# A shifted-window attention block: q and k parts in two buffers, another order of copies on SyncE's queue, and a maximum where a cast was

## The reference

```python
y = _ln(x, norm1_g, norm1_b)
y = jnp.roll(y, (-SS, -SS), axis=(1, 2))          # windows of 7 x 7 are cut from this
qkv = yw @ qkv_w.T + qkv_b
attn = jnp.einsum('bhqd,bhkd->bhqk', q * scale, k) + bias + mask
attn = softmax(attn)
o = jnp.einsum('bhqk,bhkd->bhqd', attn, v)
o = o @ proj_w.T + proj_b                         # back to the image, rolled back
x = shortcut + o
h = gelu(_ln(x, norm2_g, norm2_b) @ fc1_w.T + fc1_b)
return x + h @ fc2_w.T + fc2_b
```

## Time and profile before

| | |
|---|---|
| time, median of 3 runs (lowest to highest) | 5146.63 us (5140.37 to 5152.69) |
| the profiled execution | 5130.69 us, its span 5128.9 us |
| busy share of PE, PEld, DVE, ACT, POOL | 77%, 60%, 58%, 55%, 58% |
| mean granted clock of TensorE | 0.917 |
| SyncE's DMA queue | 429.09 MB, 38.9% of 16 DMA engines' time |
| one stack fill, one load of x | 196.0 KB each |
| the two copies of the row sums | 24.5 KB each |

### The profile page before, as it was taken

One profiled execution on the slowest core, in us unless ns is written; L12 is line 12 of the kernel. 1 busy time (PEld: TensorE's weight loads), 2 busy tenths in 40 slices (PEclk: granted clock), 3 DMA queues, 4 the chain that ended last, 5 costly groups with the idle time before them and its releaser, 6 DMA issues. The chain is left out here.

```text
span 5128.9 us, 216807 instructions
## 1 busy us (share of the span) xinstructions
PE 3941.8 (77%) x96144; PEld 3081.9 (60%) x96144; DVE 2974.2 (58%) x7839; ACT 2821.6 (55%) x3840; POOL 2995.4 (58%) x3983
## 2 busy tenths in 40 slices
PE   3777787777777787777777777778777877787777
PEld 2566666656666665665666666656666666666565
DVE  4555555556556555555555555555555555556564
ACT  1555555555555555555555555555555555555554
POOL 1566566566656656655655555566556555555665
PEclk9899989999999989999999989999999899899999
DMA  3443443444344344434433443444344334333432
GB/s 89 87 89 83 93 89 85 87 92 89 83 96 90 81 88 91 89 81 94 89 85 85 93 88 83 89 91 89 81 95 90 84 85 93 85 88 87 93 86 58
DMA packets 595395, 447.85 MB, mean 87 GB/s; under 512 B 125703, under 2 KB 594039, under 8 KB 594447
## 3 DMA queue, kind: packets, MB, share of 16 engines
q1 hardware_dynamic: 591979, 429.09, 38.9%
q10 hardware_dynamic: 2064, 3.21, 0.2%
q0 software_dynamic: 416, 1.68, 0.1%
HBM read 109.49 MB, written 51.46 MB: 31 GB/s over the span
## 5 line engine op out<-in xcount | busy, mean ns | idle before, releaser
L609 DVE TENSOR_REDUCE neg_max<-ps 113x16 f32<-113x784 f32 x1024 | 999.5, 976 | 723.7 <-PE ps L769 631.4
L430 ACT ACTIVATE probs<-ps,own 113x784 f32<-113x784 f32 x1024 | 917.7, 907 | 642.6 <-PE ps L801 586.0
L398 POOL TENSOR_TENSOR hid_lo<-probs,hid_hi 128x784 f16<-128x784 f32 x512 | 879.0, 1738 | 314.4 <-DVE hid_hi L603 314.4
L379 POOL TENSOR_SCALAR r_hi<-sums 128x98 f16<-128x98 f32 x128 | 175.2, 1368 | 1168.9 <-DVE sums L650 1168.9
L801 PE MATMUL ps<-st_q,st_k 127*49 127x49 f16 x32768 | 629.3, 186 | 130.6 <-issue 130.1
L801 PEld LDWEIGHTS ps<-st_q,st_k 127*49 127x49 f16 x32768 | 520.4, 103 | 216.7 <-issue 146.5
L492 ACT ACTIVATE k_hi<-ps,col 128x784 f16<-128x784 f32 x128 | 118.6, 926 | 927.8 <-DMA st_q<-q_lo 919.9
L769 PE MATMUL ps<-mx_k,mx_q 128*49 128x196 f16 x8192 | 546.1, 251 | 105.7 <-issue 43.8
L816 PE MATMUL ps<-probs,v_own 113*32 113x49 f32 x32768 | 515.1, 210 | 92.2 <-issue 61.3
L816 PEld LDWEIGHTS ps<-probs,v_own 113*32 113x32 f32 x32768 | 419.5, 110 | 206.2 <-issue 152.5
L848 PE MATMUL ps<-w_hi,hid_hi 128*112 128x128 f16 x3584 | 525.2, 226 | 12.9 <-issue 8.5
(11 more groups left out here) (112 smaller groups left out, 8710.0 us busy)
## 6 DMA issues: line engine op xcount, KB each, us to landing
st_k<-k_hi SPq DMA_DIRECT2D x256, 196.0 KB
st_q<-q_hi SPq DMA_DIRECT2D x256, 196.0 KB
oT_raw<-pv_sb SPq DMA_DIRECT2D x256, 196.0 KB, 6.0
x_in<-in_x SPq DMA_DIRECT2D x224, 196.0 KB
x_res<-in_x SPq DMA_DIRECT2D x224, 196.0 KB
out_y<-y_out SPq DMA_DIRECT2D x224, 196.0 KB
mx_k<-k_hi SPq DMA_DIRECT2D x512, 49.0 KB
mx_q<-q_hi SPq DMA_DIRECT2D x512, 49.0 KB
```

The source lines that it names most:

```text
L379: nc.gpsimd.tensor_scalar(r_hi[:, :, :], sums[:, :, :], 1.0, 0.0, ALU.mult, ALU.add).then_inc(s_r_hi, 1)
L398: nc.gpsimd.tensor_tensor(hid_lo[:, c, :], hid[:, c, :], hid_hi[:, c, :], ALU.subtract).then_inc(s_hid_lo, 1)
L430: nc.scalar.activation(probs[0:KP, w % 4, :].rearrange("p (b c) -> p b c", b=2), ps[0:KP, b:b + 2, 0:HB * WT], ACT.Exp, scale=own[0:KP, 2: ...
L609: nc.vector.tensor_reduce(neg_max[0:KP, :, w].rearrange("p (g e) -> p g e", g=GQ), ps[0:KP, 0:2, :].rearrange("p b (g c) -> p (b g) c", g= ...
```

## The change

Four edits:

1. `q_hi`, `q_lo`, `k_hi` and `k_lo` become two buffers each, used by turns. ScalarE's wait before `k_hi` now asks for the copies of the band before last.
2. On SyncE's queue, the last two stack fills move up behind the first four, ahead of the row sums.
3. The loads of x for band t + 3 move from behind the row sums to the end of the turn, behind the loads of `x_res`.
4. The high part of gelu's result, a cast by `tensor_copy`, becomes a `tensor_reduce` with maximum over an axis of one element, which rounds the same values to float16.

```diff
@@ buffers
-        q_hi, q_lo, k_hi, k_lo = (sb(n, [C, NW, 2, WT], F16) for n in ("q_hi", "q_lo", "k_hi", "k_lo"))
+        q_hi, q_lo, k_hi, k_lo = ([sb(f"{n}{e}", [C, NW, 2, WT], F16) for e in range(2)]
+                                  for n in ("q_hi", "q_lo", "k_hi", "k_lo"))
...
@@ SyncE
-                    fill(st_k, HIGH_ROWS, k_hi)
-                    fill(st_q, HIGH_ROWS, q_hi)
-                    fill(st_k, CROSS_ROWS[1], k_hi)
-                    fill(st_k, CROSS_ROWS[0], k_lo)
+                    fill(st_k, HIGH_ROWS, k_hi[odd(0)])
+                    fill(st_q, HIGH_ROWS, q_hi[odd(0)])
+                    fill(st_k, CROSS_ROWS[1], k_hi[odd(0)])
+                    fill(st_k, CROSS_ROWS[0], k_lo[odd(0)])
+                    fill(st_q, CROSS_ROWS[0], q_hi[odd(0)])
+                    fill(st_q, CROSS_ROWS[1], q_lo[odd(0)])
...
-                n = t + 3
-                if exists(n):
-
-                    sp.wait_ge(s_st1, n)
-                    if past(n, 1):
-                        sp.wait_ge(s_t1, n - 1)
-                    band_dmas(sp, xr, x_in[odd(3)], n, edge(n), False, s_x)
-                n = t
-                if exists(n):
-                    fill(st_q, CROSS_ROWS[0], q_hi)
-                    fill(st_q, CROSS_ROWS[1], q_lo)
...
                     band_dmas(sp, xr, x_res, n, edge(n), False, s_xres_dma)
+                n = t + 3
+                if exists(n):
+
+                    sp.wait_ge(s_st1, n)
+                    if past(n, 1):
+                        sp.wait_ge(s_t1, n - 1)
+                    band_dmas(sp, xr, x_in[odd(3)], n, edge(n), False, s_x)
...
@@ ScalarE
-                    if past(n, 0):
-                        act.wait_ge(s_mx_dma, N_MX * n)
-                        act.wait_ge(s_st_dma, N_ST * n)
-                    for j, (hi, bank, b) in enumerate(((k_hi, 0, BK), (q_hi, 6, BQ))):
+                    if past(n, 1):
+                        act.wait_ge(s_mx_dma, N_MX * (n - 1))
+                        act.wait_ge(s_st_dma, N_ST * (n - 1))
+                    for j, (hi, bank, b) in enumerate(((k_hi[odd(1)], 0, BK), (q_hi[odd(1)], 6, BQ))):
...
@@ VectorE, hid_high
-                nc.vector.tensor_copy(hid_hi[:, c, :], hid[:, c, :]).then_inc(s_hid_hi, 1)
+                nc.vector.tensor_reduce(hid_hi[:, c, :], hid[:, c, :].unsqueeze(2), AX_X, ALU.max).then_inc(s_hid_hi, 1)
```

More of the change, by code:

```diff
@@ L314, in body @@
                         sp.dma_start(mx_k[32 * e:32 * (e + 1):4, :, e, :],
-                                     k_hi[e:C:EQ, :, :, :].rearrange("c w m q -> c (w m q)")).then_inc(s_mx_dma, 16)
+                                     k_hi[odd(1)][e:C:EQ, :, :, :].rearrange("c w m q -> c (w m q)")).then_inc(s_mx_dma, 16)
                     sp.wait_ge(s_hi, 2 * n + 2)
@@ L318, in body @@
                         sp.dma_start(mx_q[edge(n)][32 * e:32 * (e + 1):4, :, :],
-                                     q_hi[e:C:EQ, :, :, :].rearrange("c w m q -> c (w m q)")).then_inc(s_mx_dma, 16)
+                                     q_hi[odd(1)][e:C:EQ, :, :, :].rearrange("c w m q -> c (w m q)")).then_inc(s_mx_dma, 16)
                 n = t - 3
@@ L657, in body @@
                 if exists(n):
-                    for j, (hi, lo, bank, b) in enumerate(((k_hi, k_lo, 0, BK), (q_hi, q_lo, 6, BQ))):
+                    for j, (hi, lo, bank, b) in enumerate(((k_hi[odd(1)], k_lo[odd(1)], 0, BK), (q_hi[odd(1)], q_lo[odd(1)], 6, BQ))):
                         dve.wait_ge(s_hi, 2 * n + j + 1)
```

## The result

| | before | after |
|---|---|---|
| median of the runs | 5149.15 us (5140.37 to 5152.69) | 5408.0 us (5403.5 to 5415.1) |
| profiled execution, span | 5130.69, 5128.9 us | 5415.1, 5413.3 us |
| mean granted clock of TensorE | 0.917 | 0.899 |

The ratio is 1.0507, with a 95% interval of 1.0488 to 1.0525. The forecast was 5255 us. The sign, the chain of waits and the range held. The size did not: about +106 us was forecast and +259 measured.

The account below looks back on a forecast made before the run. A cycle of waits repeated per band, no engine full. S 14.7 + 12.0 gives M 26.7 against 25.84: +0.86 us over 126 turns, +108 us, 5239 profiled, 5255 us median; range 5040 to 5435, with 50% on 5165 to 5360.

Parts of the forecast that it names:

- the chain of waits: Per turn: sums land later, q projection follows, one long TensorE pause, spread directly behind fc1, first row-maximum matmul behind x addition.
- The swap of waits: ScalarE's k_hi wait, 919.9 us, goes; the turn then depends on the row sums, delayed 3.8 us by two more fills.
- It is not the gain: Said of removing k_hi's 919.9 us wait: the rest of the turn passes from the last fill's landing to S.
- S: Moment VectorE gets the row sums, counted from the first fill's issue: 10.66 us before, 14.7 forecast.
- the late sums: Rival: row sums land at 16.1 us, +2.26 us a turn, 5431 us; chance 14%.
- the late turn: Second sample from the kernel before, no x left to load: 37.48 us long, S at 12.3, M at 24.0.
- x loaded last: x's two loads, 3.6 us, moved to the turn's end behind x_res: claimed to cost nothing and cover 3 us.
- S to M: From sums through q projection, spread and x addition to the first row-maximum matmul: 1.34 + 4.98 + 5.6 + 0.1 = 12.0 us.
- M: Start of the next band's first row-maximum matmul on TensorE, counted from first fill: 25.84 us before, 26.7 forecast.
- The rest of a turn: From M to the next turn's first fill: taken to follow M nearly one for one, 13.3 and 13.5 us.
- The sum: 14.7 + 12.0 = 26.7 against 25.84: +0.86 us a turn, +108 us over 126 full turns, 5255 us.
- The reduction: gelu's high part on VectorE: 976 ns against the cast's 569, 0.5 us lost there; GpSimd's r_hi 1.41 to 0.29 us.

Follow-up runs that it names:

- i_two_buffers: The kernel before with the second q and k buffers and the moved k_hi wait, nothing else: ratio 0.9651.
- d_single: The changed kernel with one buffer for each of the q and k parts and k_hi's old wait: ratio 1.0499.
- c_x_back: The changed kernel with the loads of x right behind the row sums again, as before: ratio 1.0218, 5246.66 us.
- e_oT_late: The changed kernel with the two output copies issued behind r_rows instead of right behind the sums: ratio 1.0358.
- m_x_last: i_two_buffers with the loads of x moved behind x_res as well: ratio 0.9842 to the kernel before.
- h_more_load: c_x_back with a further load of x's size behind x_res, into a buffer nobody reads: ratio 1.0380.
- b_cast: The changed kernel with gelu's high part as a cast again instead of the reduction: ratio 1.0497, 5385.59 us.
- a_sums_fifth: The changed kernel with the last two stack fills back behind the row sums, so four fills stand ahead: ratio 0.9858, 5059 us.
- j_split: The changed kernel with its queue reordered: two fills, sums, output copies, fills 3 and 4, maxima, r_rows, fills 5 and 6, x later: ratio 0.8534, 4386.67 us.
- p_split_cast: j_split with gelu's high part as a cast instead of the reduction: ratio 0.8533.
- k_four_early: j_split with fills 5 and 6 also ahead of r_rows: ratio 0.9577.

## Why the prediction was right in direction and wrong in size

- **The swap of waits: right.** k_hi's wait went, the sums' came, and TensorE's pause became a single long one before the q projection, half-clocked behind. i_two_buffers and d_single show both halves: the wait was worth 3.5% in the old order and nothing in the new one. "It is not the gain" held only for the change as a whole.
- **S, the term that was mis-sized first.** I took 14.7 and 15.49 was measured. The two fills at 1.9 us each were nearly right (4.06 us for both where x stands behind the sums, i_two_buffers and c_x_back). What I left out was what follows the sums in the queue: once x no longer stands there, the output copies do, and move beside the late fills, which costs 0.97 us against nothing there (e_oT_late) and 0.60 against x (c_x_back). Of the rivals, the late sums (S at 16.1, 5431 us) came nearest to the time. I had a row that said it, the late turn with S at 12.3 and no x, and I argued it away as the two fills "that are now the very ones that are counted".
- **x loaded last: wrong, and the step that failed.** I wrote "Cost nothing, cover 3 us" because the data are needed late and the queue is empty. I asked only who waits for x. Its place costs 2.9 points when it alone is undone (c_x_back), 1.32 us a turn where the whole sum was short by 1.39, and 1.9 when it is added to the second buffers alone (m_x_last), by two ways that I had not looked for: it was a spacer behind the sums, and its traffic now runs during the windows (h_more_load, 0.82 us a turn).
- **S to M: nearly right.** 12.0 forecast, 12.18 measured. In the turn shown, the q projection to the spread took 5.22 us (4.98 forecast) at a granted clock of 0.52, where the late turn had 0.59, and the spread to the end of the x addition 5.50 (5.6 forecast); M came right behind x, for which L767 waits 123 times.
- **The rest of a turn: wrong.** I took it as unchanged. It grew by 0.41 us, from 13.27 to 13.68. Without x in the windows it is 12.87, so the other edits had shortened it by 0.40; the second buffers did not (13.27 in i_two_buffers). The reduction may give 0.14 to 0.16 of it (changed and b_cast, a_sums_fifth and m_x_last), though j_split and p_split_cast show none; for the remainder no run tells.
- **The sum.** Against a forecast of +0.86 us a turn it was +2.25: 0.79 too little in S, 0.18 in S to M, 0.41 in the rest. That c_x_back lands on the forecast is two errors that cancel: its M is 27.16, where I had 26.7, and its rest is 0.40 shorter.
- **The reduction: right in size, no gain or loss in time.** 959 ns against 976 forecast, r_hi 0.29 us as forecast. Three pairs (changed and b_cast, a_sums_fifth and m_x_last, j_split and p_split_cast) show no difference beyond their intervals; each pair spans two groups, so half a per cent could hide there. The Trainium skill, "VectorE: DVE Perf Modes", section "Rules for kernel authors", advises against tensor_reduce on a hot path as a slow instruction. The instruction agrees (959 ns where the cast took 569); the loss that the prediction drew from it does not show in the kernel's time.

## What to carry to other kernels

Where one queue carries both the bulk fills and a small transfer that starts the next chain, send the small one first and then place each fill by when its reader needs it: with the same work, the order of SyncE's queue alone made the ratio 1.0507 or 0.8534 (changed, j_split), and putting the small transfer r_rows behind two more fills gave half of that back (k_four_early, 0.9577). A transfer that nobody waits for still has a price: ask what it stood between, what moves beside it now, and which engine works meanwhile. And when a second sample of the same cycle (here the late turn) disagrees with the first, find out what differs between them before choosing a value between.

## What the runs showed of the hardware

- Transfers can slow one that was queued ahead of them: with the sums issued at the same time in each pair (3.7 us; 4.9 us), they landed at 10.83 us with a load of x queued behind them and at 12.93 with two fills queued directly behind (i_two_buffers, m_x_last), and at 14.52 without and at 15.49 us with the output copies close behind (e_oT_late, changed). By what path is open.
- TensorE's pauses without a named releaser get longer while a load is under way: 193.4 us in the two window loops without it, 244.6 and 251.8 us with it (c_x_back; changed, h_more_load), for the same instructions.
- A cast in place of a reduction does not always hold GpSimd: its high part took 1409 ns beside casts in one order (b_cast) and 287 ns in another (p_split_cast), where the casts began later; there the casts took 944 ns on average instead of 617, one of them 2.31 us beside a GpSimd addition.
